# A graph residual-norm kernel with a windowed LSTM: reordered queues around the moves, degrees from column sums, last residual summed in PSUM

## The reference

```
A = adj + I;  deg = rowsum(A) + colsum(A) - diag(A);  dinv = 1/sqrt(deg)
Ahat = A * dinv[:,None] * dinv[None,:]
a   = Ahat @ x                                # first graph net
z   = batchnorm(relu(batchnorm(a@W1.T+b1)) @ W2.T + b2)
x1  = layernorm(x + z)
h   = relu(adj @ (x1@Wg0+bg0));  h = relu(adj @ (h@Wg1+bg1))
for p in 1..4:                                # the nodes are the time axis
    cut the time axis into windows of p steps, run an LSTM with weights p over each window,
    write its last state over the last step of the window in h
out = layernorm(x1 + h)
```

## Time and profile before

| | |
|---|---|
| median of 3 runs | 751.12 us |
| profiled execution, its own time | 748.24 us |
| its span, first to last instruction | 746.4 us |
| PE busy | 726.6 us, 97% |
| DVE busy | 644.1 us, 86% |
| ACT busy | 540.2 us, 72% |
| POOL busy | 315.2 us, 42% |
| mean granted TensorE clock | 0.995 |

### The profile page before, as it was taken

How to read it: one execution, slowest core, us unless ns; L and a number is a source line. 1 busy time by engine, 2 the same in 40 slices (tenths; PEclk the granted TensorE clock), 3 DMA queues, 4 the chain that set the end, 5 groups by cost and what they waited for, 6 DMA issues and landing times.

```text
span 746.4 us, 11167 instructions
## 1 busy us (share of the span) xinstructions
PE 726.6 (97%) x3828; PEld 414.8 (56%) x3828; DVE 644.1 (86%) x1379; ACT 540.2 (72%) x882; POOL 315.2 (42%) x289
## 2 busy tenths in 40 slices
PE   8999999999999999998999999999999999999894
PEld 6777544677777776773444444444444444554442
DVE  6888787899998989857998788899998888888987
ACT  4878998567777776748887787777767766676582
POOL 1000000168788787810000001028287385996286
PEclk9999999999999999999999999999999999999998
DMA  5643400024424233113400006051743526519012
GB/s 158 187 139 97 113 1 0 1 62 109 113 58 114 70 101 89 55 29 146 192 1 2 0 11 117 0 101 50 134 109 74 119 51 141 142 28 215 27 57 84
DMA packets 95291, 61.56 MB, mean 82 GB/s; under 512 B 25178, under 2 KB 94212, under 8 KB 94212
## 3 DMA queue, kind: packets, MB, share of 16 engines
q1 hardware_dynamic: 87844, 49.84, 23.7%
q0 software_dynamic: 7392, 11.01, 7.5%
HBM read 27.55 MB, written 16.78 MB: 59 GB/s over the span
## 4 chain that ended last, share of the span: by engine, by line
PE 60%; DVE 21%; ACT 7%; DMA 4%; SPq 3%; issue 3%; POOL 0%; POOLq 0%; DVEq 0%
PE ps L739 8%; PE ps L740 8%; PE ps L748 8%; PE ps L707 7%; PE ps L744 5%; PE ps L753 5%; PE ps L745 5%; ACT work L979 4%; PE ps L646 4%; DVE ln_stats L1263 3%; SPq L510 3%; DVE work L1227 2%; DVE store L1291 2%; DVE ring L1244 2%; DVE ring L1280 2%
## 5 line engine op out<-in xcount | busy, mean ns | idle before, releaser
L979 ACT ACTIVATE work<-ps,gate_bias 128x512 f32<-128x512 f32 x449 | 280.9, 679 | 78.7 <-PE ps L753 44.8
L739 PE MATMUL ps<-store,wih 128*128 128x512 f16 (+1 forms) x443 | 166.9, 377 | 2.4 <-ACT work L979 2.3
L740 PE MATMUL ps<-store,wih 128*128 128x512 f16 (+1 forms) x443 | 166.8, 377 | 0.0
L748 PE MATMUL ps<-store,wih 128*128 128x512 f16 (+1 forms) x443 | 156.2, 377 | 0.0
L577 POOL TENSOR_SCALAR ring<-ring,ln_mv 128x128 f32<-128x128 f32 x112 | 112.8, 1018 | 2.8 <-POOL ln_mv L565 2.7
L1227 DVE TENSOR_TENSOR work<-work 128x512 f32<-128x512 f32 (+1 forms) x129 | 88.2, 684 | 22.0 <-ACT work L986 21.9
L986 ACT ACTIVATE work<-store 128x512 f32<-128x512 f32 x97 | 60.5, 624 | 56.3 <-DVE store L1220 41.2
L588 POOL DMA_DIRECT2D ring<-turned x8 | 10.6, 1319 | 198.5 <-DMA turned<-store 190.5
L744 PE MATMUL ps<-store,whh 128*128 128x512 f16 (+1 forms) x248 | 93.3, 376 | 0.0
L745 PE MATMUL ps<-store,whh 128*128 128x512 f16 (+1 forms) x248 | 93.2, 376 | 0.0
L753 PE MATMUL ps<-store,whh 128*128 128x512 f16 (+1 forms) x248 | 93.1, 376 | 0.0
(11 more groups left out here) (140 smaller groups left out, 1274.0 us busy)
## 6 DMA issues: line engine op xcount, KB each, us to landing
ring<-in_x_dram SPq DMA_DIRECT2D x32, 256.0 KB, 2.9
ring<-in_x_dram SPq DMA_DIRECT2D x16, 512.0 KB, 5.2
x_scratch<-ring SPq DMA_DIRECT2D x16, 512.0 KB, 3.5
ring<-turned POOLq DMA_DIRECT2D x8, 768.0 KB, 6.3
ring<-x_scratch SPq DMA_DIRECT2D x5, 1024.0 KB, 6.4
store<-turned POOLq DMA_DIRECT2D x6, 768.0 KB, 6.8
out_dram<-ring SPq DMA_DIRECT2D x5, 768.0 KB, 3.9
store<-x_scratch SPq DMA_DIRECT2D x3, 1024.0 KB, 14.2
```

The source lines that it names most:

```text
L739: nc.tensor.matmul(acc(j), w_hi, x_hi, start=True, stop=False)
L740: nc.tensor.matmul(acc(j), w_lo, x_hi, start=False, stop=False)
L748: last = nc.tensor.matmul(acc(j), weights(wih, j)[0], x_lo, start=False, stop=u.first)
L979: nc.scalar.activation(acts[:, n % 2, gate, 0:u.cols], ps[:, gate_bank(q), 0:u.cols], ACT.Tanh if gate == G else ACT.Sigmoid, bias=gate_bi ...
```

## The change: what it does

1. **Loads.** The W1/W2 loads and the nine vector loads leave SP's queue and stand in ACT's, behind its first activation. SP issues `x` right behind `adj`.
2. **Degrees.** `deg = rowsum(adj without diagonal) + colsum(adj) + 1`; the column sum is one matmul of `adj` against a column of ones, the mask `off_diagonal` is one more constant. Nine DVE steps become three.
3. **PE's head.** `tmp_pp` is turned ahead of W1/W2; the vectors are turned behind the first `channels`; the dummy matmuls are 3, then 5.
4. **Moves.** SP sends the high part of a tile when `hi_done` says so, POOL adds it one unit ahead of the low part. POOL's scaling of (tile, 0) is spread over units (`PARTS`): step 1 one unit, step 2 three units later. SP's writes are at 3 units for (tile, 3), at 4 or behind the move of tile+2 for (tile, 0) (`WRITES`); (1,3) and the load of tile 7 now stand at unit 112, ahead of move 6. Reloads of tiles also wait for the adds of tiles 0 to 5.
5. **Tail.** (5,3) and (6,3) are scaled by ACT, (5,3) before was by POOL and (6,3) by DVE. The statistics of (5,3) stand behind the hidden state of unit 127, its moments inside the cell of unit 128. (6,3) is turned before the last gate of unit 128. For (7,3), PE sums the `x1` rows (through `ident`) and the hidden state in PSUM, DVE takes statistics from PSUM and scales from PSUM into the tile.

```diff
+BY_SCALARE, BY_VECTOR = [(6, 0), (5, 3), (6, 3)], [LAST]          # LAST = (7, 3)
+def scale_slots():                                                # -> PARTS
+            if piece in POOLED:
+                for k, r in enumerate(moment_rows(piece)):
+                    later = (0, 1, 3)[k] if piece[0] + 1 in MOVED else 0
+                    parts.setdefault(n + later, []).append((piece, r))
+def write_slots():                                                # -> WRITES
+            at = n + (3 if r == 3 else 4)
+            if r == 0 and move_of.get(tile + 2, at) <= n + 7:
+                at = max(at, move_of.get(tile + 2, at))
...
@@ move_rows
-                sp.wait_ge(lo_done, halves_through(...))
-                wait(sp, h_added, 32 * n)
-                for s in range(2):
+                for s, done in enumerate((hi_done, lo_done)):
+                    sp.wait_ge(done, halves_through(...))
+                    wait(sp, h_added, 16 * (2 * n - 1 + s) if n else 0)
@@ write_rows
                     sp.wait_ge(out_written[tile % X1_RING], 32 * (tile // X1_RING + 1))
+                    sp.wait_ge(h_added, 32 * (len(MOVED) - 1))
                     load_x1(tile + X1_RING)
@@ gpsimd
                 for tile in LANDS.get(n, ()):
-                    add_rows(tile)
+                    add_rows(tile, 0)
+                for tile in LANDS.get(n - 1, ()):
+                    add_rows(tile, 1)
+                for piece, r in PARTS.get(n, ()):
+                    if piece not in MOMENTS.get(n, ()):
+                        scale_row(piece, r)
@@ tensor
             keep_busy(3, 3)
+            pe.wait_ge(ld_adj, 16)
+            nc.tensor.matmul(ps[:, 1, 0:1], adj_n[:], ones[:, 0:1], start=True, stop=True).then_inc(prep_pe, 1)
             nc.tensor.transpose(ps[:, 0, 0:P], adj_n[:], ident[:]).then_inc(prep_pe, 1)
-            keep_busy(3, 2)
+            keep_busy(3, 5)
+            pe.wait_ge(prep_dve, SCALED_STEP)
+            nc.tensor.transpose(ps[:, 4, 0:P], tmp_pp[:], ident[:]).then_inc(prep_pe, 1)
             pe.wait_ge(ld_w12, 32)
...
             aggregate(0)
-            pe.wait_ge(ld_vec, 9 * 16)
-            nc.tensor.transpose(ps[:, 6, 0:P], vec_rows, ident[:]).then_inc(prep_pe, 1)
...
                 channels(c)
+                if c == 0:
+                    pe.wait_ge(ld_vec, 9 * 16)
+                    nc.tensor.transpose(ps[:, 6, 0:P], vec_rows, ident[:]).then_inc(prep_pe, 1)
...
+            def sum_last_residual():
+                for m in (0, 2):
+                    nc.tensor.matmul(last_acc(m, 2)..., ident[:], rows[:, m:m + 2, :], start=True, stop=False)
+            def sum_last_hidden():
+                pe.wait_ge(hid_done, n + 1)
+                for m in range(CB):
+                    done = nc.tensor.matmul(last_acc(m), acts[:, n % 2, O, m * P:(m + 1) * P], ident[:],
+                                            start=False, stop=(m % 2 == 1))
@@ scalar
             nc.scalar.activation(act_warm[:], ones[:, 0:1], ACT.Sigmoid)
+            act.dma_start(w12_rows[:, 0:2, :], ...); act.dma_start(w12_rows[:, 2:4, :]..., W2)
+            nine act.dma_start(vec_rows[...], ...)
@@ vector
+            link(nc.vector.tensor_tensor(tmp_pp[:], adj_n[:], off_diagonal[:], ALU.mult))
+            link(nc.vector.reduce_sum(rsum, tmp_pp[:], AX_X))
+            dve.wait_ge(prep_pe, 1)
+            step(nc.vector.scalar_tensor_tensor(deg, ps[:, 1, 0:1], 1.0, rsum, ALU.add, ALU.add))
...
                 for m in range(CB):
+                    row = rows[:, m, :]
+                    if (tile, r) == LAST:
+                        dve.wait_ge(last_summed, 1 + m // 2)
+                        row = last_acc(m)
...
+                if n == end - 1:
+                    end_row_stats(*BY_SCALARE[1])
+            end_row_stats(*TAIL[0])
+            end_moments(TAIL[0])
+            end_row_stats(*LAST)
+            end_moments(LAST)
+            end_scale(*LAST)
```

More of the change, by code:

```diff
@@ L584, in add_rows, with raise_rows @@
                 pool.wait_ge(x1_loaded[tile % X1_RING], 16 * (tile // X1_RING + 1))
[L585 to L590, removed]
+                pool.wait_ge(h_moved[s], 16 * CB * (n + 1))
+                wait(pool, h_added, 16 * (2 * n + s))
+                nc.gpsimd.dma_start(rows, h_rows[:, s, :, :].rearrange("p (m r) d -> p m (r d)", r=3),
+                                    accum_op=ALU.add).then_inc(h_added, 16)
+            def raise_rows(piece):
                 n = MOMENT_ORDER.index(piece)
@@ L600, in scale_rows @@
                 pool.wait_ge(end_step, 4 * (n + 1))
                 pool.wait_ge(end_rstd, n + 1)
[L602 to L611, removed]
@@ L612, in scale_rows @@
-                last.then_inc(end_scaled, 1)
+                for m in range(CB):
+                    row = x1_tile[tile % X1_RING][:, 4 * m + r, :]
+                    k = r * CB + m
+                    last = nc.gpsimd.tensor_scalar(row, row, mv[:, 1, k:k + 1], mv[:, 4, k:k + 1],
+                                                   ALU.subtract, ALU.mult)
+                if r == moment_rows(piece).stop - 1:
+                    last.then_inc(end_scaled, 1)
             for n in range(N_EARLY, len(UNITS)):
@@ L864, in mix_gnn @@
                     last.then_inc(gnn_summed, 1)
+            def sum_last_residual():
+                tile, r = LAST
+                pe.wait_ge(x1_loaded[tile % X1_RING], 16 * (tile // X1_RING + 1))
+                pe.wait_ge(end_added, len(TURN_ORDER) - 2)
+                pe.wait_ge(gate_done, GATE0[len(UNITS) - 1])
+                rows = x1_tile[tile % X1_RING].rearrange("p (m r) d -> p r m d", r=4)[:, r, :, :]
+                for m in (0, 2):
+                    nc.tensor.matmul(last_acc(m, 2).rearrange("p (m d) -> p m d", d=P), ident[:], rows[:, m:m + 2, :],
+                                     start=True, stop=False)
+            def sum_last_hidden():
+                n = len(UNITS) - 1
+                pe.wait_ge(hid_done, n + 1)
+                for m in range(CB):
+                    done = nc.tensor.matmul(last_acc(m), acts[:, n % 2, O, m * P:(m + 1) * P], ident[:],
+                                            start=False, stop=(m % 2 == 1))
+                    if m % 2 == 1:
+                        done.then_inc(last_summed, 1)
             def turn_h(tile, r):
@@ L1061, in _ @@
                     end_scale(*SCALES[n])
+            for piece in BY_SCALARE[1:]:
+                end_scale(*piece)
         @block.vector
@@ L1074, in link @@
                 dve.wait_ge(prep_dve, steps[0])
-            rsum, csum, diag, deg, dinv = (small[:, k:k + 1] for k in range(5))
+            rsum, deg, dinv = (small[:, k:k + 1] for k in (0, 3, 4))
+            dve.wait_ge(consts_done, N_CONSTS - 2)
+            dve.wait_ge(ld_adj, 16)
+            link(nc.vector.tensor_tensor(tmp_pp[:], adj_n[:], off_diagonal[:], ALU.mult))
+            link(nc.vector.reduce_sum(rsum, tmp_pp[:], AX_X))
+            dve.wait_ge(prep_pe, 1)
+            step(nc.vector.scalar_tensor_tensor(deg, ps[:, 1, 0:1], 1.0, rsum, ALU.add, ALU.add))
+            assert steps[0] == DEG_STEP
             dve.wait_ge(consts_done, N_CONSTS)
-            dve.wait_ge(ld_adj, 16)
             link(nc.vector.tensor_tensor(a_norm[:], adj_n[:], ident[:], ALU.add))
[L1080 to L1089, removed]
+            dve.wait_ge(prep_pe, 2)
+            step(nc.vector.tensor_copy(adjT[:], ps[:, 0, 0:P]))
             dve.wait_ge(dinv_done, 1)
@@ L1104, in agg_lo @@
                     .then_inc(agg_lo_done, 1)
-            dve.wait_ge(prep_pe, 4)
-            step(nc.vector.tensor_copy(vec[:], ps[:, 6, 0:P]))
-            assert steps[0] == VEC_STEP
-            agg_lo(0)
             for h in range(H1):
@@ L1112, in _ @@
             dve.wait_ge(prep_pe, 5)
-            link(nc.vector.tensor_copy(row_sums[:], ps[:, 5, 0:P]))
+            step(nc.vector.tensor_copy(row_sums[:], ps[:, 5, 0:P]))
             assert steps[0] == RS_STEP
+            agg_lo(0)
+            agg_lo(1)
+            dve.wait_ge(prep_pe, 6)
+            link(nc.vector.tensor_copy(vec[:], ps[:, 6, 0:P]))
+            assert steps[0] == VEC_STEP
             for b in range(CB):
@@ L1321, in end_scale @@
             def end_scale(tile, r):
-                piece = (tile, 3 if r == 3 else 0)
-                n = MOMENT_ORDER.index(piece)
+                n = MOMENT_ORDER.index((tile, r))
                 dve.wait_ge(end_step, 4 * (n + 1))
@@ L1328, in end_scale @@
                     k = r * CB + m
-                    last = nc.vector.tensor_scalar(row, row, end_mv[:, tile, 1, k:k + 1],
+                    last = nc.vector.tensor_scalar(row, last_acc(m), end_mv[:, tile, 1, k:k + 1],
                                                    end_mv[:, tile, 4, k:k + 1], ALU.subtract, ALU.mult)
-                if r == moment_rows(piece).stop - 1:
-                    last.then_inc(tail_scaled, 1)
+                last.then_inc(tail_scaled, 1)
```

(11 more changed lines are left out.)

134 lines of the change are left out of this document (77 added, 57 removed).

## The result

The changed kernel takes 744.05 us, the median of 6 runs (743.92 to 746.57), against 750.85 us (749.05 to 752.79, 6 runs) before: a ratio of 0.9917 with a 95% interval of 0.9899 to 0.9935. That is 6.8 us less by the medians, and 6.2 by the ratio (4.9 to 7.6). 746.7 us was forecast, with a range of 745.2 to 749.3. The forecast gain was 4.45 us. The two profiled executions differ by less: 748.24 before, 743.92 after, 4.32 us (spans 746.4 and 742.2). So the sum held between the two traces, and not between the medians. One of the six executions after, 746.57 us, lies 2.2 us or more above the others; no trace shows it.

What follows compares the result with a forecast made beforehand. TensorE (PE) was taken to bound the kernel, with time to gain only where it idles. Middle 2.30, head 1.50 and tail 0.65 made 4.45 us, subtracted from the median 751.12: 746.7 us, range 745.2 to 749.3.

Steps and rivals of the forecast that it cites:

- the last of the sum: Final step: subtract the 4.45 us gain from the runs' median, 751.12, rather than the profiled 748.24, giving 746.7.
- Middle: LSTM stage: earlier adds of tile 6 remove VectorE's 2.86 us stall; gain 2.30 us, bounds 0 and 2.5.
- the hole of the earlier trace: LSTM stage, TensorE starts at 699.66 and 702.18: 2.30 us lost behind VectorE's late hidden, 2.14 us of it idle.
- nothing: LSTM stage: claim that nothing else is late next on TensorE once tile 6's stall goes; slack 0.56 us better than zero.
- the later load of tile 6: SP's queue: waiting for tile 5's adds moves this load some 5 us later, with over 20 us until its add.
- the removed company: LSTM stage: the write of (1,3) and tile 7's 1 MB load no longer run beside tile 6's second add.
- Head: Before the chunk loop's steady work: second aggregate at 7.95 instead of 9.59; net gain 1.5 us.
- the bounds: Head: W1/W2 landing between 5.0 and 7.1 us, taken as 5.8.
- rival (d): Head: ACT pays more per DMA issue than SP, making the kernel slower, 753.6 us at 1.15 each; chance 0.05.
- its cadence: Chunk loop: TensorE starts a chunk every 2.19 us; a break in the first chunks would show the prediction wrong.
- Tail: After TensorE's last matmul: (7,3) summed in PSUM drops end_add and shortens the chain; gain 0.65 us, bounds 0.2 and 1.0.
- an estimated 0.28: Tail: cost in us of the last four scalings losing double rate from PSUM, left out of the sum.

Runs made afterwards that it cites:

- e2: Only part 4 (split moves and adds, spread scaling, write slots, wait ahead of reloads) on the kernel before: 745.96 us, ratio 0.9943.
- e9: The kernel before, no edit, profiled again: 750.9 us median of 8 runs, profiled execution 750.4 us.
- e4: Only part 5 (the tail) on the kernel before: 751.03 us, ratio 1.0003; profiled execution 751.74 us.
- e5: The kernel before with one added line, SP's wait for the adds of tiles 0 to 5 ahead of each reload: 747.47 us, ratio 0.9954.
- e6: e5 plus SP's writes in the new slots, without split moves or spread scaling: 745.79 us, ratio 0.9928.
- e7: The kernel before with split moves and adds and spread scaling, old write slots, no wait ahead of reloads: 746.44 us, ratio 0.9937.
- e11: The kernel after, W1/W2 turned behind the first aggregate, two dummies fewer, wait for W1's fp16 parts ahead of the first channels: 743.49 us, ratio 0.991.
- e1: The kernel before, no edit, run again: 751.47 us median of 10 runs, profiled execution 748.47 us.
- e3: Only parts 1 to 3 (loads, degrees, TensorE's head) on the kernel before: 747.82 us, ratio 0.9975.

## Why the prediction was wrong

The step that failed is the last of the sum: "it lies 2.88 under the median of the runs, and I subtract from the median". I took the 2.88 us between the profiled execution and the median for an offset that the changed kernel would share. It was stalls, present in most executions and absent in the one I read, and on the very path that the change mends. With the moves alone changed (e2) the gain is 4.8 us by the medians where the trace had 2.30 to give. The changed kernel's profiled execution lies 0.13 under its median.

- *Middle*, 2.30 forecast: the hole of the earlier trace rows is closed as reasoned, 2.30 us in the traces. What was missing is the stall at tile 5, which costs 2.3 us in e9, and the halved clock behind the hole, 1.5 us in e4. By time and clock some 40 of the 75 executions have the first and 45 the second. The trace of the cheap execution did show the sign: VectorE waits 1.06 us for tile 5's add, which the prediction passed over as "nothing" since no TensorE hole followed. A wait of a transfer that is just absorbed, beside runs that spread over 1.6 us, was a stall waiting to happen. I took the later load of tile 6 as free, which it is, and saw no gain in it; by e5 it takes away the stall, and by the counts above that is about half of the surplus.
- *Which edit of the middle:* I gave the weight to the earlier high part and the spread scaling, and called the removed company a help. e6 and e7 show that each alone closes the hole.
- *Head*, 1.50 forecast, 1.12 in the trace. `tmp_pp` was turned at 5.82, as forecast, right behind the dummies. W1/W2 were mis-sized: I took 3.1 us to land after an issue at 2.7; the second was issued at 2.23 and landed 4.1 us later, for TensorE's first turn at 6.34, inside the bounds. That moved the first `aggregate` to 7.24 instead of 6.75, and the second from 7.95 to 8.36. Taking both the landing and the wait for W1's parts off TensorE's path (e11) gives 0.35 us; VectorE's first pieces and the last vector load stand right behind them. ACT's issues take 0.24 to 0.54 us each, against the 0.25 to 0.46 of SP, so rival (d) had no ground. The loop kept its cadence, 2.19 us.
- *Tail*, 0.65 forecast. From the start of the last `hidden` to the end of the last scaling it is 6.69 us before (736.94 to 743.63) and 6.18 after (733.20 to 739.38): 0.51. The last `hidden` itself starts 3.74 us earlier, where head and hole explain 3.42; the remaining 0.32 goes with the new order of statistics and moments on VectorE, by subtraction only. Together 0.83.
- The four scalings out of PSUM take 1.37 us against the 1.12 of the earlier trace rows: 0.25 us. The Trainium skill, "VectorE: DVE Perf Modes", section "Why PSUM operands drop a tier", holds fp32 work with a PSUM operand to the single rate; the prediction priced that from rows at an estimated 0.28 and left it out of the sum. The trace agrees, with 0.25.

The sum of the parts in one trace is 2.30 + 1.12 + 0.83 = 4.25 us of span, against 746.4 - 742.2 = 4.2. The forecast of 4.45 is so near to it partly by luck: the head gave 0.38 less and the tail 0.18 more. What stays open: why the transposes of tile 5 land in two kinds (3.25 to 3.43 us after the last issue in the traces of before, e1 and e3, 5.55 and 5.59 in e4 and e9), that is, where the stall originates; what decides whether the clock falls behind the hole, since no trace of the kernel before shows it; and what the one execution of 746.57 us after the change had, at a mean clock of 0.996.

## What to carry to other kernels

When a profiled execution is faster than nearly all timed ones, it doesn't show the usual execution: compare the mean granted clocks as well as the times, profile again until one near the median is read, and take a change's gain as a range from the one to the other. Here a spread of over 4 us, on one core alone, came from a wait that was only sometimes absorbed and from a clock that only sometimes fell; look for transfers that land just in time. A large load issued beside a small transfer that somebody waits for should be made to wait or be put ahead of it: one line and changed write slots (e6) gave 5.4 us here.

## What the runs showed of the hardware

TensorE stood for 2.66 us in one execution (e4) and ran at half the granted clock for 3.4 us, from before the end of the hole; in three others it stood 2.14 to 2.37 us at the same place at the full clock. If the low mean clocks are such falls, 45 of 75 executions of the kernel before had one, so no length of hole is shown to decide it. An accumulating add of 768 KB issued by GpSimd lands after 5.7 to 6.4 us alone and after 9.3 to 11.8 us when a 1 MB load is issued within about 1.2 us of it (before, e5, e7, e9). In the head the same dummy matmuls reached the full clock as early as 5.0 us (e4) and as late as 7.45 us (e7) after the start, by the trace's record of the granted clock, in kernels with the same head as before; the first `aggregate` of these kernels starts between 6.95 (e4) and 7.41 (e5).
